# Last layer norm of a mixture-of-experts layer begun two tiles before the experts end, and gelu written twice by ScalarE

## The reference

```
x = layernorm(x + attention(x))                      # D = 256, H = 16 heads
logits = xf @ wr + br                                # xf: 4096 tokens x 256
topk_vals, topk_idx = top_k(logits, 2)
gates = softmax(topk_vals)
h = gelu(einsum('nd,edh->enh', xf, w1) + b1[:, None, :], approximate=False)   # E = 4, hidden 1024
y = einsum('enh,ehd->end', h, w2) + b2[:, None, :]
out = einsum('nk,nkd->nd', gates, y_sel - c_sel + c_sum)   # c: what an expert gives for no input
x = layernorm(x + out)                               # (x - mean) / sqrt(var + 1e-5)
```

## Time and profile before

| what | value |
|---|---|
| median of 3 runs | 1062.55 us (1061.18 to 1064.93) |
| the profiled execution, its own time | 1066.83 us |
| span of the profiled execution | 1065.1 us |
| busy PE, DVE, ACT, POOL | 929.2, 835.0, 495.6, 430.5 us |
| mean granted clock of TensorE | 0.958 of full |

### The profile page before, as it was taken

How to read it: one execution, slowest core, us unless ns; L and a number is a source line. 1 busy time by engine, 2 the same in 40 slices (tenths; PEclk the granted TensorE clock), 3 DMA queues, 4 the chain that set the end, 5 groups by cost and what they waited for, 6 DMA issues and landing times.

```text
span 1065.1 us, 26698 instructions
## 1 busy us (share of the span) xinstructions
PE 929.2 (87%) x8002; PEld 676.0 (63%) x8003; DVE 835.0 (78%) x2990; ACT 495.6 (47%) x1045; POOL 430.5 (40%) x376
## 2 busy tenths in 40 slices
PE   3688999997989989998896799899999999999920
PEld 1244656555656566565664577788889778988920
DVE  4637789797898988988987789887777887777737
ACT  3256554553555635555355545343444333333304
POOL 6418055383453653735537512223222442322321
PEclk8789999999999999999999989999999999999975
DMA  4785103224133032230133432223223332232356
GB/s 141 250 213 147 32 22 105 80 70 118 35 91 92 25 120 59 62 119 2 51 111 120 159 110 41 41 52 47 46 42 61 81 59 45 50 50 50 50 124 222
DMA packets 61535, 90.33 MB, mean 85 GB/s; under 512 B 8620, under 2 KB 51136, under 8 KB 60384
## 3 DMA queue, kind: packets, MB, share of 16 engines
q1 hardware_dynamic: 45832, 62.73, 19.9%
q0 software_dynamic: 14304, 21.90, 11.2%
q10 hardware_dynamic: 1280, 4.19, 1.1%
HBM read 52.80 MB, written 35.86 MB: 83 GB/s over the span
## 4 chain that ended last, share of the span: by engine, by line
PE 55%; DVE 25%; issue 6%; DMA 6%; SPq 4%; ACT 2%; DVEq 1%; POOL 0%; ACTq 0%; POOLq 0%
PE sm L1375 6%; PE st L1375 5%; PE ms L1160 5%; PE sm L1388 5%; PE pv L1388 5%; PE sm L1242 5%; PE st L1202 4%; PE pv L1222 4%; DVE junk L1780 4%; PE ms L1300 3%; DVE arena_b L1942 3%; DVE arena_b L1940 2%; PE ms L1272 2%; DVE beaten L1727 2%; PE st L1204 2%
## 5 line engine op out<-in xcount | busy, mean ns | idle before, releaser
L1780 DVE CUSTOM_DVE_ANT_0 junk<-sm,mask_ts 128x512 bf16<-128x512 f32 (+3 forms) x512 | 220.1, 485 | 61.1 <-PE sm L1242 58.7
L900 POOL DMA_INDIRECT sums<-arena_b x70 | 112.6, 1609 | 294.7 <-DVE arena_b L1968 280.6
L1028 ACT ACTIVATE arena_b<-st 128x512 f32<-128x512 f32 x320 | 180.2, 598 | 101.6 <-PE st L1204 100.2
L1202 PE MATMUL st<-arena_a 128*128 128x384 f16 (+3 forms) x512 | 126.5, 304 | 24.1 <-ACT arena_b L1028 16.7
L1242 PE MATMUL sm<-arena_a 128*128 128x512 f16 (+3 forms) x512 | 112.9, 309 | 18.0 <-DVE maxes L1780 11.9
L1942 DVE TENSOR_TENSOR arena_b<-arena_b 128x256 f16<-128x256 f32 x280 | 120.2, 429 | 9.6
L1099 ACT ACTIVATE arena_b<-sm,arena_b 128x256 f32<-128x256 f32 x140 | 66.1, 474 | 125.5 <-PE sm L1375 107.0
L1375 PE MATMUL st<-arena_b,arena_a 128*128 128x256 f16 x840 | 115.6, 275 | 7.7 <-DVE arena_b L1659 6.9
L1940 DVE CAST arena_b<-arena_b 128x256 f16<-128x256 f32 x280 | 88.8, 317 | 38.5 <-ACT arena_b L1099 36.9
L1388 PE MATMUL pv<-arena_a,arena_b 128*128 x864 | 118.0, 275 | 0.0
L1099 ACT ACTIVATE arena_b<-st,arena_b 128x256 f32<-128x256 f32 x140 | 65.9, 473 | 111.0 <-PE st L1375 95.9
(11 more groups left out here) (292 smaller groups left out, 1675.0 us busy)
## 6 DMA issues: line engine op xcount, KB each, us to landing
arena_b<-slots SPq DMA_DIRECT2D x37, 260.0 KB, 2.8
arena_a<-w SPq DMA_DIRECT2D x8, 1024.0 KB, 6.8
arena_b<-x_tr SPq DMA_DIRECT2D x8, 512.0 KB, 4.2
q_rows<-arena_b SPq DMA_DIRECT2D x32, 128.0 KB
k_rows<-arena_b SPq DMA_DIRECT2D x32, 128.0 KB
arena_a<-q_rows SPq DMA_DIRECT2D x32, 128.0 KB
arena_a<-k_rows SPq DMA_DIRECT2D x32, 128.0 KB
res<-x_tok POOLq DMA_DIRECT2D x8, 512.0 KB, 4.7
```

What stands on the lines that cost most here:

```text
L900: pool.indirect_dma_start(sums, bass.IndirectOffsetOnAxis(ap=token_now[:, 1 - par, m:m + 1], axis=0), y_out[1 - par][:, m, :], None, compu ...
L1028: act.activation(probs[:, q, :], st_ps[piece % 2][:, :], ACT.Exp, scale=SCORE_SCALE).then_inc(exp_done, 1)
L1202: pe.matmul(out[:, at:at + width], ks[:, h % 2, h // 2, s * P:(s + 1) * P], qs[:, h // 2, s * P:T], start=m == 0, stop=False, skip_group_c ...
L1780: last = dve.tensor_tensor_reduce(junk[:, n % 3, at:at + width], sm_ps[n % 3][:, at:at + width], mask_ts[:, T - width:T], 1.0, NEG, ALU.ad ...
```

## The change

**Gelu.** ACT now computes each piece twice from PSUM: once to fp32 (`g_32`) and once to fp16 (`g_hi`). The cast on DVE is gone; DVE keeps the subtraction. PE's reuse of a PSUM bank, and the loads of the next biases, wait for the second gelu (`ghi_done`) instead of the first.

**Finish.** The last two tiles (33 and 34, KEPT = 2) are no longer added to `sums` in HBM. SP loads `sums` as soon as the adds of tile 32 have landed, into SBUF buffers of the attention stage that are free by then (`homes`), and all 32 blocks are normalised and stored, though the rows of tokens in tiles 33 and 34 aren't complete. These at most 512 rows are completed on chip: POOL gathers their rows of `sums` by token; PE and DVE build a 0/1 matrix `same` that tells which of the 512 rows belong to the same token; PE multiplies it with `y_out` of the two tiles, so that a token in both tiles gets both parts; DVE adds, these 4 blocks are normalised too, and POOL writes them by token over the rows of `out` after all stores have landed (a second copy of a token, or an empty row, goes to spare rows behind the output). The 1/sqrt now is Ln and Exp on ACT with one Newton step on DVE, and for blocks 0 to 7 ACT takes the sums and squares. The scaling is divided over ACT, POOL and DVE by a table.

The core of the diff:

```diff
-GROUPS = [(0, 8), (8, 16), (16, 24), (24, 28), (28, BLOCKS)]
+GROUPS = [(8, 16), (16, 24), (0, 8), (24, BLOCKS), (BLOCKS, BLOCKS + KEPT_BLOCKS)]
+UNITS_STORED = (2, 3, 4, 0, 5, 1, 6, 7)
+SCALED_BY = {0: "aaaa", 1: "aaaa", 2: "pppp", 3: "pppp", 4: "ppdp", 5: "ppdp", 6: "aapd", 7: "aapd", 8: "dada"}
...
@@ ffn_schedule
-            with eng.Fori(0, (TILES - UNROLLED) // 2) as k:
+            with eng.Fori(0, (FIRST_KEPT - UNROLLED) // 2) as k:
                 tile(Count(k, 2, UNROLLED), UNROLLED % 2, True, True)
                 tile(Count(k, 2, UNROLLED + 1), 1 - UNROLLED % 2, True, True)
+            for t in range(FIRST_KEPT, TILES):
+                tile(t, t % 2, True, True)
...
@@ SP, finish
-            sp.wait_ge(added, 32 * TILES)
-            for g, (first, end) in enumerate(GROUPS):
-                sp.dma_start(fin[:, first:end, :], sums_by_block[:, first:end, :]).then_inc(fin_in[g], 16)
+            sp.wait_ge(added, 32 * FIRST_KEPT)
+            for n in (1, 0, 2, 3, 4):
+                first, home = homes[n]
+                sp.dma_start(home, sums_by_block[:, first:first + home.shape[1], :]).then_inc(fin_in[n], 16)
...
@@ POOL, after the last tile
+            pool.wait_ge(kept_set, KEPT)
+            pool.wait_ge(added, 32 * FIRST_KEPT)
+            for n in range(KEPT_BLOCKS):
+                pool.indirect_dma_start(rows_kept[:, n, 0:D], None, sums, bass.IndirectOffsetOnAxis(ap=token_kept[:, n // 2, n % 2:n % 2 + 1], axis=0)).then_inc(kept_moved, 16)
+            places_of_kept_rows()
...
+            pool.wait_ge(out_s, 16 * len(UNITS_STORED))
+            for n in range(KEPT_BLOCKS):
+                pool.indirect_dma_start(out, bass.IndirectOffsetOnAxis(ap=token_out[:, n // 2, n % 2:n % 2 + 1], axis=0), rows_kept[:, n, 0:D], None).then_inc(kept_moved, 16)
...
@@ ACT, tile
                         act.activation(g_32[:, hc % 4, :], u_bank(hc)[:, 0:ROWS], ACT.Gelu, bias=b1_now[:, par, hc:hc + 1],
                                        scale=1.0 / W_SCALE).then_inc(gelu_done, 1)
-                        if hc == 4:
+                        if hc == 0 and later(t, 2):
+                            act.wait_ge(y_ready, n_of(t - 1))
+                        act.activation(g_hi[par][:, hc, :], u_bank(hc)[:, 0:ROWS], ACT.Gelu, bias=b1_now[:, par, hc:hc + 1],
+                                       scale=1.0 / W_SCALE).then_inc(ghi_done, 1)
+                        if hc == 4 and t != TILES - 1:
                             rows_high(t + 1, 1 - par)
...
@@ ACT, finish (SUMMED_BY_ACT = 2, the blocks 0 to 7; KEPT_GROUP = 4)
+            act.preload_act_table_set("natural_log_exp_and_others")
+            sums_of(SUMMED_BY_ACT)
+            seed(0)
+            squares_of(SUMMED_BY_ACT)
+            seed(1)
+            seed(2)
+            scaled(2)
+            seed(3)
+            scaled(3)
+            seed(KEPT_GROUP)
+            scaled(KEPT_GROUP)
...
@@ PE, after the last second layer
+                for k in range(KEPT):
+                    pe.wait_ge(yg_done, 2 * (FIRST_KEPT + k + 1))
+                    for n in range(2):
+                        for to in range(KEPT_BLOCKS):
+                            last = pe.matmul(st_ps[to // 2][:, to % 2 * D:(to % 2 + 1) * D], same[:, 2 * k + n, to * P:(to + 1) * P], y_out[(FIRST_KEPT + k) % 2][:, n, :],
...
@@ DVE, tile
-                        dve.tensor_copy(g_hi[par][:, hc, :], g_32[:, hc % 4, :]).then_inc(ghi_done, 1)
                         dve.wait_ge(ghi_done, n_of(HC * t + hc + 1))
                         dve.tensor_tensor(g_lo[par][:, hc, :], g_32[:, hc % 4, :], g_hi[par][:, hc, :], ALU.subtract).then_inc(hid_done, 1)
...
@@ DVE, finish (aggregates, squares_in, deviations: the variance, and one Newton step on what ACT gives)
+            deviations(0)
+            statistics(16, 24)
+            aggregates(1)
+            statistics(24, 28)
+            squares_in(2)
+            deviations(1)
+            deviations(2)
+            scaled(1)
+            statistics(28, 32)
+            aggregates(3)
+            kept_rows()
+            statistics(BLOCKS, BLOCKS + KEPT_BLOCKS)
+            deviations(3)
+            scaled(3)
```

284 lines of the change are left out of this document (206 added, 78 removed).

## The result

The changed kernel takes 1054.74 us (median of 11 runs, 1047.76 to 1058.35) against 1064.84 of the kernel before (median of 11, 1057.16 to 1068.66). The ratio is 0.9914, 95% interval [0.9895, 0.9933]: 9.2 us faster, between 7.1 and 11.2. A gain of 17.4 had been forecast. The level of 1054.7 lies inside the range of the prediction, the gain is about half of what it named. The profiled execution took 1054.74 us, its span is 1053.1 (before: 1066.83 and 1065.1).

A forecast was written before the change was run, and what follows sets the result against it. PE was taken to set the pace in the experts' stage, losing 17.9 us to late DVE, with a 46 us finish behind the last matmul. Savings of 9.2 + 8.2 = 17.4 us gave 1045.1 us, range 1035.5 to 1055.

The forecast's parts named there:

- The ten waits for rows: Experts' stage: PE's 8.6 us of waits for rows of `slots`, put down to late DVE; 5.0 us to be gained.
- The short waits for low parts: Experts' stage: PE's two shorter waits for the next tile's low parts, 1.7 us, all to be gained.
- the first tile: Experts' stage: 5.16 us of idle PE while POOL slows DVE's casts and subtractions; 1.7 us to be gained.
- The wait for zs: Experts' stage: PE's 2.4 us wait for a result of the attention stage's remains; 1.3 us to be gained.
- The table change on ACT: Experts' stage, tile 13: one more gelu between three table loads and `rows_high`; 0.5 us to be lost.
- The clock: Experts' stage: TensorE at half clock behind the first wait; 2.6 us might come back, not counted in the sum.
- steps 1 to 4: Finish: loads, statistics, sums, scalings up to the last store, issued at 1045.4, 33 us after SP's load.
- step 5: Finish: the last store lands, POOL writes four times 128 rows; end at 1056.9, 8.2 us saved.
- the rival with reloads: Finish: ACT reloads tables for each logarithm and exponential, costing 7.7 us, total 1052.8; chance 0.02.
- The slower rival: Experts' loop: row loads meet POOL's adds and land late, 0.8 us lost per tile, total 1071; chance 0.04.
- the experts' stage gives little: Experts' stage gains only 3 us, as slow landings keep the waits for rows; total 1051.3; chance 0.18.
- the finish gives 3: Finish gains only 3 us, as accumulation is dear and DVE waits on ACT; total 1050.3; chance 0.15.

The follow-up runs named there:

- drain: Changed kernel with DVE waiting, ahead of subtractions 1 to 7 of a tile, for the end of its own last subtraction; 1048.22 us in a single run.
- tokens_later: Changed kernel with a tile's tokens copied aside, then copied on only ahead of the scaling by the gates; 1042.67 us in a single run.
- pool_last: Kernel before with one more wait: POOL waits at its end for the landing of the last store; 1062.83 us in a single run.

## Why the prediction was right or wrong

The direction was right, and the likeliest case promised nearly twice the gain. By the stretches of the traces, with the kernels of one kind averaged (stage before 411.8, 406.2, 409.2, mean 409.1; with the gelu part 402.9, 405.8, 404.0, 402.4, 402.4, mean 403.5), the experts' stage gave 5.6 us of 9.2, and the end 5.1 of 8.2 (46.0 and 45.7 before, 40.5 to 41.0 after). That is 10.7, and the ratio says 7.1 to 11.2; the 5.6 rest on single traces that scatter by 3 to 6 among kernels of one kind. Point by point:

- **The ten waits for rows, forecast 5.0, measured nothing.** 8.6, 4.9 and 5.6 us in the three kernels with the cast, 8.4, 7.2, 6.0, 6.0 and 6.1 without. This is the step that failed: from "all of them have DVE behind them" to rows that come earlier when DVE does. In tiles 2 to 5 of the kernel before the premise was so, for DVE was late there itself (it waited 0.2 us in all for adds). But directly behind that cover stood the wait for POOL's adds: with DVE early, `row_gates` waited for them, 10.0 us in five places. One of them is the add slowed to 5.37 us beside the unbroken stretch that the removed casts left behind, another the eight writes to `slots` ahead of the adds. drain shows the first link, tokens_later the wait. The six later waits, of which the prediction took under half, it put down to table changes and slow landings; with the wait for adds gone two waits of 1.5 us in all are left. The wait was named in the code shown ahead of the prediction, and was not priced.
- **The short waits for low parts, forecast 1.7, and the first tile, 1.7.** Together the waits for low parts were 6.9, 7.5 and 8.0 before, and 3.3, 3.3, 4.7, 3.3 and 3.3 after: 3.9 gained, 3.4 forecast. A subtraction did meet POOL's long operation in the first tile, as feared.
- **The wait for zs, forecast 1.3, gave 2.6**: 2.6 to 2.8 before, 0 to 0.5 after.
- **The table change on ACT, forecast -0.5, cost 0.6**: 0.6 to 1.2, in every kernel.
- **The clock.** The first six matmuls behind the shorter wait ran at the granted clock of 1 (0.83 us for 6 in the changed kernel, 1.46 in the earlier trace rows), and the granted clock fell to 0.50 (1.2 GHz) from 613.7 to 617.1. PE's busy time in the stage is 391.9 on average before and 391.6 after, so in sum it gave next to nothing, and leaving it out did no harm. But it was not idle: four of the five kernels with the gelu part had a further stretch at 0.50 behind a wait for rows, and without those waits 3.6 us came back (tokens_later).
- **Finish, steps 1 to 4: right as a sum.** The last store leaves 32.2 us behind the first load, 33.2 forecast. Single parts were off and cancelled: blocks 0 to 7 land after 12.3 us instead of 11.7; a sum takes ACT 0.40 and the next starts 0.40 after it, with reading the accumulator (0.18) beside it, instead of 0.55.
- **Finish, step 5: mis-sized by 5.3 us.** From the last store to the end 11.5 were forecast (3.8 to land, 3.9 for three writes and their issue, 3.8 for the last) and 16.8 measured. The parts named came to 10.7 (4.3, 3.96 and a landing of 2.4); behind them stand 6.1 us in which POOL's program ends, a term that the sum did not have. In the kernel before it began 1.0 us ahead of the last store, with POOL's last scaling, so that it did not show as idle time of its own; pool_last shows it. The load also came 8.2 us ahead of the last matmul's end instead of 6.9, which gave 1.3 back. One load of tables, hidden, as the forecast took it, and none between logarithm and exponential: the rival with reloads is out. The Trainium skill (ScalarE: Activation LUTs, Table sets) has it so.
- **The slower rival** did not come: row loads in the loop landed in 2.7 to 3.3 us.

What happened was thus a bit of two rivals at once, "the experts' stage gives little" and "the finish gives 3", each for another mechanism than the one written beside it. They were given their chances one by one and never the case of both.

## What to carry to other kernels

When an engine that was late is relieved, list what its first instruction behind the relieved stretch waits for, on all its semaphores, and when each of them is due: the next wait is already in the code. Here moving one copy behind a wait that stood there anyway made the stage 8 us shorter in its traced execution, where the whole gelu part had given 5.6. And let the engine whose program ends slowly end early: give its last wait to another.
